# The expert loop of a ViT tower on one core: plain fp32 first product, three-pass second product

## The reference

```
scores = jax.nn.softmax(xf @ gate_w.T, axis=-1)
_, idx = jax.lax.top_k(scores + gate_b, K)            # K = 6 of E = 64 experts, at most CAP = 128 rows each
xb = jnp.zeros((E, CAP, D), xf.dtype).at[se, pos].set(xf[tok], mode='drop')
h = jax.nn.silu(jnp.einsum('ecd,eid->eci', xb, w1)) * jnp.einsum('ecd,eid->eci', xb, w3)   # I = 176
yb = jnp.einsum('eci,edi->ecd', h, w2)
y = jnp.zeros_like(xf).at[tok].add(contrib * wf[:, None])
z = jax.nn.silu(xf @ ws1.T) * (xf @ ws3.T) @ ws2.T
return (y + z).reshape(shape)
```

## Time and profile before

| | |
|---|---|
| median of 3 runs | 662.71 us (661.63 to 662.99) |
| the profiled execution's own time | 662.18 us |
| span of that execution (first to last instruction) | 660.1 us |
| busy share over the span: PE, DVE, ACT, POOL | 79%, 66%, 56%, 35% |
| expert loop, first to last gather and put | 443.6 us to 632.4 us |

### The profile page before, as it was taken

How to read it: one execution, slowest core, us unless ns; L and a number is a source line. 1 busy time by engine, 2 the same in 40 slices (tenths; PEclk the granted TensorE clock), 3 DMA queues, 4 the chain that set the end, 5 groups by cost and what they waited for, 6 DMA issues and landing times.

```text
span 660.1 us, 9760 instructions
## 1 busy us (share of the span) xinstructions
PE 523.0 (79%) x3182; PEld 439.7 (67%) x3182; DVE 438.9 (66%) x918; ACT 366.4 (56%) x894; POOL 234.1 (35%) x234
## 2 busy tenths in 40 slices
PE   4945954266745989999999999998999988989835
PEld 3723843023323989999999888886888867777724
DVE  5949897999998246544555612477787876865516
ACT  1637645255446657667767534725776766765600
POOL 2021001023424321022221041236777777777720
PEclk9975888578675889999999999998999999999969
DMA  8970000009000000000000001012677776676457
GB/s 279 383 250 0 1 0 0 0 5 305 22 2 0 25 1 25 25 25 25 25 1 1 1 1 49 21 26 66 207 224 213 232 211 197 209 215 196 136 221 260
DMA packets 44053, 67.43 MB, mean 102 GB/s; under 512 B 11149, under 2 KB 27142, under 8 KB 43876
## 3 DMA queue, kind: packets, MB, share of 16 engines
q1 hardware_dynamic: 36836, 64.62, 30.6%
q0 software_dynamic: 7168, 2.20, 1.6%
HBM read 66.81 MB, written 17.72 MB: 128 GB/s over the span
## 4 chain that ended last, share of the span: by engine, by line
PE 43%; DVE 29%; DMA 10%; issue 7%; ACT 5%; POOL 4%; SPq 1%; POOLq 0%; DVEq 0%; ACTq 0%
PE ps L725 6%; PE ps L727 5%; PE ps L726 5%; PE ps L936 5%; PE ps L894 5%; DMA region<-x_rows,region 4%; PE ps L1089 4%; DVE region L1725 3%; DMA region<-y_rows 2%; PE ps L925 2%; DMA y_rows<-region 2%; PE ps L908 2%; PE ps L1062 2%; POOL y_rows L685 2%; DVE region L1669 2%
## 5 line engine op out<-in xcount | busy, mean ns | idle before, releaser
L1725 DVE TENSOR_TENSOR region<-ps,region 32x136 f32<-32x136 f32 x128 | 38.1, 297 | 73.9 <-PE ps L894 72.3
L725 PE MATMUL ps<-nTh,high 128*128 128x272 f32 (+2 forms) x248 | 75.4, 304 | 8.7 <-ACT region L1300 8.7
L676 POOL DMA_INDIRECT region<-x_rows,region x64 | 72.7, 1136 | 20.3 <-issue 14.7
L685 POOL DMA_INDIRECT y_rows<-region x64 | 71.4, 1116 | 23.4 <-issue 11.3
L635 POOL COPY region<-region 32x544 f32<-32x544 f32 x32 | 26.1, 815 | 134.0 <-DVE region L1744 132.5
L726 PE MATMUL ps<-nTl,high 128*128 128x272 f32 (+2 forms) x248 | 72.7, 293 | 0.0
L1864 DVE TENSOR_TENSOR w_low<-region,high 128x704 fp32r<-128x704 f32 x64 | 57.4, 898 | 15.2 <-ACT high L1400 15.2
L1089 PE MATMUL ps<-region 88*128 88x256 f32 x256 | 65.7, 379 | 0.0
L727 PE MATMUL ps<-nTh,pairs_low 128*128 128x272 f32 x192 | 56.5, 294 | 0.0
L725 PEld LDWEIGHTS ps<-nTh,high 128*128 128x128 f32 (+2 forms) x248 | 47.2, 190 | 11.1 <-ACT region L1300 10.3
L1400 ACT ACTIVATE high<-region 128x704 fp32r<-128x704 f32 x64 | 50.2, 784 | 0.0
(11 more groups left out here) (249 smaller groups left out, 1356.2 us busy)
## 6 DMA issues: line engine op xcount, KB each, us to landing
region<-moe_w SPq DMA_DIRECT2D x64, 352.0 KB
region<-moe_w SPq DMA_DIRECT2D x64, 176.0 KB
y_rows<-zrow SPq DMA_DIRECT2D x1, 6528.0 KB, 25.3
region<-y_rows SPq DMA_DIRECT2D x8, 768.0 KB, 9.4
region<-wqkv SPq DMA_DIRECT2D x8, 384.0 KB, 3.0
region<-ffn_w SPq DMA_DIRECT2D x2, 1024.0 KB, 8.0
region<-patches SPq DMA_DIRECT2D x3, 384.0 KB, 8.3
region<-patches SPq DMA_DIRECT2D x1, 1152.0 KB, 10.7
```

The costliest lines, as they stand in the source:

```text
L676: nc.gpsimd.indirect_dma_start(out=xb[m8], out_offset=None, in_=x_rows, in_offset=bass.IndirectOffsetOnAxis(ap=sloti[:, at:at + 1], axis=0 ...
L685: nc.gpsimd.indirect_dma_start(out=y_rows, out_offset=bass.IndirectOffsetOnAxis(ap=sld[m8], axis=0), in_=yb[m], in_offset=None, bounds_che ...
L725: nc.tensor.matmul(out, parts_a[0], parts_b[0], start=first, stop=False)
L1725: last = V.tensor_tensor(sc[r, s0:s0 + 8, 0:T].rearrange("p (a b) t -> p a b t", a=4), ps[r, 4:8, 0:4 * GW].rearrange("p a (b h t) -> p a ...
```

## The change

The three-pass scheme moves from the first product to the second one. The first product reads w13 and the transposed rows as they are, in plain fp32. The second product gets high and low parts: ACT writes the high part of w2 (88x512) and of the gated rows, DVE writes the low part of the gated rows and that of w2, the latter in two halves (88x256 each) at two places of its step. PE's semaphore waits follow. The weights' high part is now made in step n for expert n, behind a wait for the second product of expert n-2, since there are two buffers of it. The buffers of the split moved along with it (w2_l over w2, w2_h in the place of w13_h).

```diff
@@ pe_step
-                    pe.wait_ge(s_xbl, n + 1)
-                    pe.wait_ge(s_w1l, n + 1)
+                    pe.wait_ge(s_xbT, n + 1)
+                    pe.wait_ge(s_w13[m], 4 * (n - m) + 16)
                     need(pe, s_eh, n - 1)
                     for c in range(DC):
-                        mm = product(ps[:, 2 + m % 2, 0:2 * EI], (xbT_h[m % 2][:, c, :], xbT_l[m % 2][:, c, :]),
-                                     (w13_h[m % 2][:, c, :], w13_l[m][:, c, :]), c == 0, c == 1)
+                        mm = nc.tensor.matmul(ps[:, 2 + m % 2, 0:2 * EI], xbT[m % 2][:, c, :], w13[m][:, c, :],
+                                              start=(c == 0), stop=(c == DC - 1))
                     mm.then_inc(s_eh13, 1)
                 if 0 <= n - 1 < E:
                     e, k = n - 1, (m - 1) % 4
                     pe.wait_ge(s_eh, e + 1)
-                    need(pe, s_ehT, e)
+                    need(pe, s_ehl, e)
...
                 if 0 <= n - 2 < E:
                     e, k = n - 2, (m - 2) % 4
-                    pe.wait_ge(s_ehT, e + 1)
-                    pe.wait_ge(s_w2[k], 4 * (e - k) + 16)
+                    pe.wait_ge(s_ehl, e + 1)
+                    pe.wait_ge(s_w2l, 2 * (e + 1))
                     need(pe, s_yb, e - 1)
                     for c in range(2):
-                        mm = nc.tensor.matmul(ps[:, 5 + 2 * (k % 2), 0:D], ehT[k % 2][:, c, :], w2[k][:, c, :],
-                                              start=(c == 0), stop=(c == 1))
+                        mm = product(ps[:, 5 + 2 * (k % 2), 0:D], (ehT_h[k % 2][:, c, :], ehT_l[k % 2][:, c, :]),
+                                     (w2_h[k % 2][:, c, :], w2_l[k][:, c, :]), c == 0, c == 1)
@@ act_step
-                if 0 <= n + 2 < E:
-                    e, k = n + 2, (m + 2) % 4
-                    act.wait_ge(s_w13[k], 4 * (e - k) + 16)
-                    need(act, s_eh13, e - 1)
-                    nc.scalar.activation(w13_h[k % 2], w13[k], ACT.Copy).then_inc(s_w1h, 1)
+                if 0 <= n < E:
+                    act.wait_ge(s_w2[m], 4 * (n - m) + 16)
+                    need(act, s_y, n - 1)
+                    nc.scalar.activation(w2_h[m % 2], w2[m], ACT.Copy).then_inc(s_w2h, 1)
@@ dve_step
-                if 0 <= n + 1 < E:
-                    e, k = n + 1, (m + 1) % 4
-                    dve.wait_ge(s_w1h, e + 1)
-                    V.tensor_tensor(w13_l[k], w13[k], w13_h[k % 2].bitcast(F32), ALU.subtract).then_inc(s_w1l, 1)
-                    dve.wait_ge(s_xbT, e + 1)
-                    need(dve, s_eh13, e - 1)
-                    V.tensor_tensor(xbT_l[k % 2], ps[:, k % 2, 0:2 * P].rearrange("p (c n) -> p c n", c=DC),
-                                    xbT_h[k % 2].bitcast(F32), ALU.subtract).then_inc(s_xbl, 1)
+                if 0 <= n - 1 < E:
+                    k = (m - 1) % 4
+                    dve.wait_ge(s_w2h, n)
+                    V.tensor_tensor(w2_l[k][:, 0, :], w2[k][:, 0, :], w2_h[k % 2][:, 0, :].bitcast(F32),
+                                    ALU.subtract).then_inc(s_w2l, 1)
...
+                if 0 <= n - 1 < E:
+                    e, k = n - 1, (m - 1) % 4
+                    dve.wait_ge(s_ehT, e + 1)
+                    need(dve, s_y, e - 1)
+                    V.tensor_tensor(ehT_l[k % 2], ps[0:EH, 4, 0:2 * P].rearrange("p (c n) -> p c n", c=2),
+                                    ehT_h[k % 2].bitcast(F32), ALU.subtract).then_inc(s_ehl, 1)
+                    V.tensor_tensor(w2_l[k][:, 1, :], w2[k][:, 1, :], w2_h[k % 2][:, 1, :].bitcast(F32),
+                                    ALU.subtract).then_inc(s_w2l, 1)
```

More of the change, by code:

```diff
@@ L238, in build @@
         w13 = [reg1.cut([P, DC, 2 * EI]) for _ in range(4)]
+        w2_at = reg1.at
         w2 = [reg1.cut([EH, 2, D]) for _ in range(4)]
@@ L268, in build @@
         eh = [reg2.cut([P, EI]) for _ in range(2)]
-        ehT = [reg2.cut([EH, 2, CAP]) for _ in range(2)]
+        xbT = [reg2.cut([P, DC, CAP]) for _ in range(2)]
         yb = [reg2.cut([P, D]) for _ in range(4)]
@@ L300, in build @@
         gate_l = cuts(at_word(R1 + gate_at, DC * E, "gate_low"), 0, [DC, E])
-        w13_low = at_word(R1 + w13_at, 4 * DC * 2 * EI, "w13_low")
-        w13_l = [cuts(w13_low, k * DC * 2 * EI, [DC, 2 * EI]) for k in range(4)]
-        xbT_h, xbT_l = ([cuts(pairs_low, (2 * u + k) * DC * CAP, [DC, CAP]) for k in range(2)] for u in range(2))
+        w2_low = at_word(R1 + w2_at, 4 * 2 * D, "w2_low")
+        w2_l = [cuts(w2_low, k * 2 * D, [2, D])[0:EH] for k in range(4)]
+        ehT_h, ehT_l = ([cuts(pairs_low, (2 * u + k) * 2 * CAP, [2, CAP])[0:EH] for k in range(2)] for u in range(2))
         high = at_word(R2 + high_at, 2 * 3 * DC * P, "high")
@@ L307, in build @@
         gate_h = cuts(high, 2 * DC * SI, [DC, E])
-        w13_h = [cuts(high, k * DC * 2 * EI, [DC, 2 * EI]) for k in range(2)]
+        w2_h = [cuts(high, k * 2 * D, [2, D])[0:EH] for k in range(2)]
         x_rows = nc.dram_tensor("x_rows", (N, XW), F32, kind="Internal").ap()
@@ L412, in build @@
         s_xbT = sem("s_xbT")
-        s_xbl = sem("s_xbl")
-        s_w1h = sem("s_w1h")
-        s_w1l = sem("s_w1l")
+        s_ehl = sem("s_ehl")
+        s_w2h = sem("s_w2h")
+        s_w2l = sem("s_w2l")
         s_eh13 = sem("s_eh13")
@@ L1059, in pe_step @@
                     pe.wait_ge(s_got[k], 4 * (e - k) + 16)
-                    need(pe, s_xbl, e - 1)
+                    need(pe, s_xbT, e - 1)
                     for c in range(DC):
@@ L1383, in act_step @@
                     need(act, s_eh13, e - 1)
-                    nc.scalar.activation(xbT_h[k % 2], ps[:, k % 2, 0:2 * P].rearrange("p (c n) -> p c n", c=DC),
+                    nc.scalar.activation(xbT[k % 2], ps[:, k % 2, 0:2 * P].rearrange("p (c n) -> p c n", c=DC),
                                          ACT.Copy).then_inc(s_xbT, 1)
@@ L1393, in act_step @@
                     need(act, s_y, e - 1)
-                    nc.scalar.activation(ehT[k % 2], ps[0:EH, 4, 0:2 * P].rearrange("p (c n) -> p c n", c=2),
+                    nc.scalar.activation(ehT_h[k % 2], ps[0:EH, 4, 0:2 * P].rearrange("p (c n) -> p c n", c=2),
                                          ACT.Copy).then_inc(s_ehT, 1)
-                if 0 <= n + 2 < E:
-                    e, k = n + 2, (m + 2) % 4
-                    act.wait_ge(s_w13[k], 4 * (e - k) + 16)
-                    need(act, s_eh13, e - 1)
-                    nc.scalar.activation(w13_h[k % 2], w13[k], ACT.Copy).then_inc(s_w1h, 1)
+                if 0 <= n < E:
+                    act.wait_ge(s_w2[m], 4 * (n - m) + 16)
+                    need(act, s_y, n - 1)
+                    nc.scalar.activation(w2_h[m % 2], w2[m], ACT.Copy).then_inc(s_w2h, 1)
             run_steps(act_step)
```

## The result

The changed kernel takes 651.1 us (median of 6 runs, 649.8 to 659.98), the kernel before 662.17 (6 runs, among them the three of the table of before), a ratio of 0.984 [0.981, 0.986]. It is 11 us faster where I had forecast 6. The profiled execution has a span of 648.7 us and a time of its own of 650.81, so it is 11.4 under that of before. One thing comes ahead of all else: this was measured where the kernel before takes 662 us. Executions that are over 1.5% slower than the fastest of their kernel stay out of the ratios but not out of the medians, and the only profile of the kernel before from those two chips is of such an execution.

A forecast was written before the change was run, and what follows sets the result against it. POOL was taken to bound the expert loop, with PE tying after the change: 662.18 - 9 (POOL's stalls) + 2.7 (tie, late w2, slot search) = 655.9, given as 656.3 us; range 650 to 665.

The forecast's parts named there:

- PE never holds POOL up: Expert loop: second product's starts free, new waits covered, POOL alone sets the end; -9 to -12 us; chance 0.12.
- my tie: Expert loop, first three blocks at least: PE at 2.74 us per expert, POOL at 2.73; waits booked at 1.5 to 2 us.
- the head: Start of the expert loop: the rows' low part leaves the chain before the first product; priced at nothing.
- POOL's stalls: Expert loop: gathers and puts held under L1864 lose 13.0 us; shorter DVE instructions leave 3.9, saving 9 us.
- The estimate by chance: Expert loop: POOL instructions start at random under DVE's two halves, window times mean wait; 0.07 us per expert, 3.9 in all.
- Two short blocks are as bad as one long: Expert loop: PE and POOL lock in phase, short DVE pieces hit more often; stalls 7.4 us, time 660 to 664; chance 0.20.
- PE's step: Both products in the expert loop: first +0.22, second -0.09 us; net +0.10 per expert, bare step 2.28 to 2.38 us.
- the slower rival: Second product becomes the bound, its six passes waiting for operands or weights; +0.3 us per expert gives about 668; chance 0.16.
- late w2: Expert loop: w2's load must land two steps after issue, not four; a few late by up to 0.6 us; booked 0.5.
- the slot search: Behind L1887 once a block, it delays the next expert's parts; 0.2 to 0.5 us a block, 0.5 booked in the sum.
- The end: End of the loop: expert 63's chain gets 0.9 us longer, covered by the 1.4 us before the last put; no cost.
- within 0.2%: Whole kernel: the change moves nothing measurable; chance 0.12 in the summary, 0.06 at the rival, as part of the partial case.

The follow-up runs named there:

- two pieces of 518 ns: The kernel before with the subtraction L1864 (128x704) cut into two back-to-back pieces of 128x352; 656.75 us, ratio 0.988.
- four of 334 ns: The kernel before with the subtraction L1864 (128x704) cut into four back-to-back pieces of 128x176; 657.5 us, ratio 0.991.
- run 12: The changed kernel with w2's split one step later, both low halves back to back at the end of DVE's step; 658.55 us, 0.991 to the kernel before.

## Why the prediction was right, and where it was off

The direction and the main mechanism held, and the median is inside the range. The gain was undersized by 5 us, so that the time fell not in the likeliest part (653 to 660) but where I had put the rival "PE never holds POOL up" (650 to 653), and that rival also describes this loop better than my tie does. It was not that alone: with the head as I had booked it, at nothing, the time would have been 653.2. Term by term, in the profiled executions and from put 0 to put 54 where nothing else is said:

- *POOL's stalls, -9 forecast, -10.5 measured.* Their kind, their end 0.90 us behind the DVE instruction and the longest (1.26 us, at most 1.35 forecast) came out as said; 1.8 us are left and not 3.9. The estimate by chance (window times mean wait) is fair where the phase is mixed: 6.3 us for two pieces of 518 ns by the same formula, measured 7.2; 3.7 for four of 334 ns, measured 4.4. In the changed kernel chance was kinder than that: where the halves fall against POOL decides, as run 12 shows with 5.2 us for the same halves. That part of the gain was luck. The rival "Two short blocks are as bad as one long" is the effect that run 12 has in part.
- *PE's step, +0.10 forecast.* The bare step went from 2.27 to 2.34, +0.07; silu 8 to 24 from 42.2 to 43.4 us, +0.08 per expert. The six one-pass matmuls are 0.12 us apart (0.117 forecast) and the weight loads of 0.19 us do not pace them, so the slower rival is refuted at its own step on this chip:

```profile
542.73 0.28 PE L727 MATMUL ps<-w_low,pairs_low 88*128 88x256 f32 x1
542.73 0.19 PEld L728 LDWEIGHTS ps<-high,pairs_low 88*128 88x128 f32 x1
542.85 0.28 PE L728 MATMUL ps<-high,pairs_low 88*128 88x256 f32 x1
```

- *The tie, late w2 and the slot search, +2.7 forecast, +0.7 measured.* Together they are what the pace less stretch rose by (143.8 to 144.4), and POOL's waits for ACT's copy rose by just that (0.4 to 1.1 us). The two engines are as close as I had said only in the first blocks: PE's pace from silu 8 to 24 is 2.72 us per expert, POOL's from put to put 2.71. From silu 24 to 40 PE is at 2.53, without a hole, and makes up what it had fallen behind. That each wait in a tie is lost for both was argued, and booked too high. Late w2 was priced at 0.5 and is 0: by its packets w2 is in at least 0.9 us before L1400 starts on it, and L1400 showed no wait for DMA. The step behind the slot search grew by 0.13 to 0.20 us in the first three blocks, some 0.1 us more than the bare step did, where I had booked 0.2 to 0.5 a block.
- *The head, 0 forecast, -2.1 measured.* Leaving the chain in front of the first product was named in the part on DVE and priced at nothing. At the loop's start nothing covers it, and the granted clock falls behind PE's long wait there, which the prediction had no part for.
- *The end, "covered", +0.6 measured.* The cover of 1.4 us was there because POOL was late. With POOL faster, two puts near the end wait for ACT's copy, 0.62 and 1.13 us where 0.30 is usual; before, put 54's own stretch of 0.6 us stood in this part.

```profile
615.33 0.98 POOL L686 DMA_INDIRECT y_rows<-region  x1 [0.62 <-ACT region L1380]
617.44 0.98 POOL L686 DMA_INDIRECT y_rows<-region  x1 [1.13 <-ACT region L1380]
```

-10.54 + 0.66 - 2.09 + 0.59 = -11.38, the difference of the two profiled executions. What the prediction also had no part for is that the bound can differ from chip to chip: the whole argument was read from one execution, in which no engine sat idle without a releaser. And its chances for "within 0.2%" do not agree, 0.06 at the rival and 0.12 in the summary; the other numbers of its sum come out as it says.

## What to carry to other kernels

An indirect DMA issued by GpSimd was held here by two kinds of VectorE instruction, a tensor_tensor with both inputs in SBUF and a tensor_scalar from SBUF, until shortly before their end, and not by others; find out in the timeline which ones do it. If such a queue sets the pace, cut or shorten those instructions before touching anything else, and try the pieces apart (back to back they cost 5.2 us, apart 1.8). When a stall goes, ask at once which engine ties next, and look at the first and last iteration too, where no other work covers a shorter or longer chain. Time a gain of 1 to 2% on more than one chip, since here it was there on one and gone on another.

## What the runs showed of the hardware

- A gather or put is held until 0.12 us before the end of the DVE instruction it runs into, by tensor_tensor with two SBUF inputs and by tensor_scalar with one (0.53 us for 704 columns), but not by MAX8 from SBUF (1.29 us) nor by instructions with an input from PSUM. Between two pieces back to back it mostly gets through: the longest was 1.38 us with pieces of 0.52, not the 1.68 of the earlier trace rows, but one put of 1.66 us was held across pieces of 0.33.
- It goes the other way too: beside POOL's tensor_tensor a DVE instruction of 0.89 us took 1.47, and one of 0.53 took 1.11.
- The granted clock fell to its lower level for 3.4 us at the head of the loop behind a wait of PE of 1.91 us, and did not fall where the first product did not wait for the split.
- The kernel before takes 662 to 665 us in three sets of runs and 681 in two others, on other chips; the changed kernel takes 651 and 688, with a mean clock of 0.905 and 0.899 in the profiled executions and all of their difference behind put 0. Idle times of over 0.6 us with no releaser are in all profiles from the slower chips and in none from the others.
